# The last stage of a transformer chain merged into the six-layer stage, and cross-attention products on four row groups

## What is computed

```python
# six layers, 16 heads of 8, context of 77 tokens
for i in range(6):
    x = x + attn(rope(adaln(x) @ q), rope(adaln(x) @ k), adaln(x) @ v) @ so      # self
    x = x + attn(rope(adaln(x) @ cq), rope(context @ ck), context @ cv) @ co     # cross
    x = x + gelu(adaln(x) @ f1 + b1) @ f2 + b2
# last block, on h = layernorm(x) of that sum
scores = sigmoid(h @ gate_w)                     # 64 experts in 8 groups
# the best 4 groups, of them the best 8 experts; weights normalised, times 2.5
y = sum_e w_e * ((silu(h @ Wg_e) * (h @ Wu_e)) @ Wd_e)  + shared expert
x = x + y
```

## Time and profile before

| | us |
|---|---|
| median of 3 runs | 2892.53 (2888.77 to 2898.36) |
| the profiled execution's own time | 2894.29 |
| its span | 2892.5 |
| TensorE busy | 2426.3 (84%), mean granted clock 0.856 |
| VectorE, ScalarE busy | 1662.8 (57%), 1171.5 (41%) |
| stage C, about 1100 to 2642 | 1542 |
| stage D with store, 2642 to the end | 251 |

### The profile page before, as it was taken

One profiled execution on the slowest core, in us unless ns is written; L12 is line 12 of the kernel. 1 busy time (PEld: TensorE's weight loads), 2 busy tenths in 40 slices (PEclk: granted clock), 3 DMA queues, 4 the chain that ended last, 5 costly groups with the idle time before them and its releaser, 6 DMA issues. The chain is left out here.

```text
span 2892.5 us, 32350 instructions
## 1 busy us (share of the span) xinstructions
PE 2426.3 (84%) x11288; PEld 956.9 (33%) x11288; DVE 1662.8 (57%) x3709; ACT 1171.5 (40%) x1984; POOL 148.1 (5%) x143
## 2 busy tenths in 40 slices
PE   5999788789996974888888989889798888874799
PEld 2333243433332651233223233222322323222244
DVE  4666758346565576764674574576458347622544
ACT  2333232112222332563655466365456537622121
POOL 0000000011110012000000000000000000001000
PEclk9999988679997896896888699598879859955899
DMA  3000000200000011000100010010001000002000
GB/s 131 1 1 0 1 1 0 103 1 1 1 1 1 1 43 44 23 1 22 39 1 23 1 39 1 22 39 1 23 1 39 1 22 23 1 0 91 0 1 8
DMA packets 38098, 54.35 MB, mean 19 GB/s; under 512 B 5137, under 2 KB 34610, under 8 KB 36402
## 3 DMA queue, kind: packets, MB, share of 16 engines
q1 hardware_dynamic: 37938, 52.28, 5.7%
HBM read 32.34 MB, written 0.52 MB: 11 GB/s over the span
## 5 line engine op out<-in xcount | busy, mean ns | idle before, releaser
L2175 DVE TENSOR_REDUCE C_nm<-ps 128x1 f32<-128x512 f32 x768 | 501.0, 685 | 260.0 <-PE ps L1675 257.6
L2034 ACT ACTIVATE C_prob<-ps 128x512 f32<-128x512 f32 x768 | 430.2, 594 | 198.7 <-PE ps L1695 193.7
L1675 PE MATMUL ps<-C_ks,C_qs 62*128 62x512 bf16 x768 | 275.3, 439 | 52.7 <-DVE C_nm L2175 34.4
L1695 PE MATMUL ps<-C_qs,C_ks 64*128 64x512 bf16 x768 | 256.8, 408 | 43.3 <-ACT C_prob L2034 40.0
L1710 PE MATMUL ps<-C_prob,C_va 128*32 128x512 f32 x1536 | 218.4, 642 | 6.3 <-ACT C_prob L2034 6.3
L2127 ACT ACTIVATE C_u<-ps,C_biasx 77x512 f32<-77x512 f32 x192 | 120.8, 678 | 162.2 <-PE ps L1818 161.8
L1814 PE MATMUL ps<-C_qx,C_kc 32*77 32x512 f32 x384 | 160.6, 922 | 15.2 <-ACT C_u L2127 11.2
L1675 PEld LDWEIGHTS ps<-C_ks,C_qs 62*128 62x128 bf16 x768 | 59.8, 96 | 273.0 <-DVE C_nm L2175 173.0
L714 DVE TENSOR_REDUCE A_nm<-ps 128x2 f32<-128x1024 f32 x64 | 77.6, 1212 | 112.5 <-PE ps L497 112.4
L1695 PEld LDWEIGHTS ps<-C_qs,C_ks 64*128 64x128 bf16 x768 | 56.7, 94 | 255.8 <-ACT C_prob L2034 182.2
L1791 PE MATMUL ps<-C_kc,C_qx 32*128 32x308 f32 x384 | 98.8, 593 | 31.4 <-DVE C_nmx L2266 13.7
(11 more groups left out here) (366 smaller groups left out, 3972.7 us busy)
## 6 DMA issues: line engine op xcount, KB each, us to landing
C_qs<-C_parts SPq DMA_DIRECT2D x72, 128.0 KB, 2.4
C_ks<-C_parts SPq DMA_DIRECT2D x72, 128.0 KB, 2.4
C_w<-in_C_w SPq DMA_DIRECT2D x6, 1090.0 KB, 5.2
D_w<-in_D_ew SPq DMA_DIRECT2D x8, 768.0 KB, 11.4
B_w<-in_B_ew SPq DMA_DIRECT2D x8, 514.0 KB, 10.7
normw_later<-in_norm_w SPq DMA_DIRECT2D x1, 2304.0 KB
A_w<-in_A_w SPq DMA_DIRECT2D x2, 1024.0 KB, 11.9
A_w<-in_A_w SPq DMA_DIRECT2D x2, 768.0 KB, 8.3
```

The costliest lines, as they stand in the source:

```text
L1675: pe.matmul(ps[:, S_BANK + hp, :], lhsT=qs[side(hp, MAX_ROW), b, 2 * q + pq, t * P:(t + 1) * P], rhs=ks[side(hp, MAX_ROW), b, 2 * q + pq, ...
L1695: pe.matmul(ps[:, ST_BANK + hp, :], lhsT=ks[side(1 - hp, HALF), b, 2 * q + pq, kt * P:(kt + 1) * P], rhs=qs[side(1 - hp, HALF), b, 2 * q + ...
L2034: act.activation(prob[:, kt % 2, pq, 1 - hp, :], ps[:, ST_BANK + hp, :], ACT.Exp, scale=SCALE)\
L2175: dve.tensor_reduce(nm[:, q % 2, t, pq, hp:hp + 1], ps[:, S_BANK + hp, :], AX.X, ALU.max, negate=True).then_inc(max_done, 1)
```

## The change

1. Stage D as a stage is gone. `experts_plan` makes a list of extra steps with slots, and `merged` sorts them into the queues of TensorE, ScalarE and VectorE among the units' steps. For batch 0 they start right after unit 10's `FEED_BACK` on VectorE: residual add and norm as one step, then router in 12 parts, gates, and from 300 slots on an expert step every 30 slots; unit 11 ends 913 slots after unit 10. Batch 1's norm and router start after unit 11's `FEED_BACK`, its experts after batch 0's last. Each batch runs its 33 steps by itself; gate, up, spread and down use one bank each: 2, 3, 4 and 1.
2. Memory is shared: `qs`, `ks`, `va` become one buffer `attn`, into which the expert weights are loaded (two DMAs of eight pairs for each batch's half, each after the last weighing of unit 10 or 11). Router tiles lie in `first`, `cos`, `sin`; expert products in `prob`. SP issues these loads after all its other work. GpSimd builds `d.sel` ahead of unit 11's `VX`.
3. `cross_max` and `cross_T` take four row groups at once: 4 steps of four products each in place of 8 of two. r = 0 and 1 go to the banks of `scores` (0, 1) or `scores_T` (2, 3), the others to the ring; in unit 11 only r = 0 does. The heads are laid out anew (`headx`), so that an Exp group of four is one `weigh_x`.
4. `apply` moves from ScalarE to VectorE, as `tensor_scalar` with mean and rstd; the step that made `m.lnu` goes.
5. Banks 0 to 3 are counted by `filled` and `emptied` as the ring is. The slot tables are new throughout, `WINDOW` is 1214.

```diff
-WINDOW = 1155
+WINDOW = 1214
@@ tables, excerpts (b = 0, then b = 1) @@
-     "MAX_X": [1845, 1871, 1895, 1911, 1931, 1949, 1973, 1989],
-     "ST_X": [2048, 2069, 2091, 2124, 2159, 2188, 2222, 2262],
+     "MAX_X": [1935, 1974, 2007, 2047],
+     "ST_X": [2105, 2141, 2200, 2379],
...
-     "ST_X": [1786, 1808, 1829, 1858, 1886, 1923, 1951, 1982],
+     "ST_X": [1898, 1950, 2017, 2080],
@@ VECTOR @@
-     "FEED_BACK": [2572],
+     "FEED_BACK": [2715],
...
-     "FEED_BACK": [2295],
+     "FEED_BACK": [2414],
@@ SCALAR, b = 1 @@
-     "EXP_X": [1800, 1821, 1843, 1872, 1900, 1937, 1964, 1996],
+     "EXP_X": [1923, 1975, 2031, 2094],
...
-     "GELU": [2198, 2219, 2227, 2237],
+     "GELU": [2318, 2340, 2348, 2356],
@@ new @@
+D_STRIDE = 30
+D_EXPERTS = 300
+STEPS_D = PAIR_D + 1
+def experts_plan():
+    last = [(UNITS - B + b) * WINDOW + VECTOR[b]["FEED_BACK"][0] for b in range(B)]
+    plan = {"PE": [], "ACT": [], "DVE": []}
+    begin = 0
+    for b in range(B):
+        at = last[b]
+        plan["DVE"].append((at + 6, "norm", b, 0))
+        plan["PE"].append((at + 66, "turn_norm", b, 0))
+        plan["ACT"].append((at + 76, "copy_norm", b, 0))
+        plan["PE"].append((at + 84, "logits", b, 0))
+        plan["ACT"].append((at + 94, "sigmoid", b, 0))
+        for i in range(ROUTE_PARTS):
+            plan["DVE"].append((at + 104 + 14 * i, "route", b, i))
+        plan["PE"].append((at + 104 + 14 * ROUTE_PARTS, "turn_gates", b, 0))
+        for half in range(2):
+            plan["DVE"].append((at + 114 + 14 * ROUTE_PARTS + 28 * half, "split_gates", b, half))
+        begin = max(begin, at + D_EXPERTS)
+        for e in range(STEPS_D + 1):
+            place = begin + e * D_STRIDE
+            plan["PE"].append((place, "step", b, e))
+            if e < STEPS_D:
+                plan["ACT"].append((place + 10, "silu", b, e))
+                plan["DVE"].append((place + 20, "step", b, e))
+        begin += STEPS_D * D_STRIDE + 4
+        plan["DVE"].append((begin + 16, "take_sum", b, 0))
+        plan["PE"].append((begin + 24, "turn_sum", b, 0))
+        plan["DVE"].append((begin + 32, "add_sum", b, 0))
+    return plan
@@ cross_T (cross_max alike, with S_BANK and 4 * CTX columns) @@
-                    banks = [fill(("stx", c, i, gh)) for gh in range(2)]
+                    banks = [take(("stx", c, q, r), (ST_BANK if c < UNITS - 1 else S_BANK) + r) for r in range(fixed(c))]
+                    banks += [fill(("stx", c, q, r)) for r in range(fixed(c), 4)]
+                    for r in range(4):
+                        rows = slice(32 * r, 32 * r + 32)
+                        pe.matmul(ps[0:CTX, banks[r], :], lhsT=cross.k[rows, c, q, :], rhs=qx[rows, :],
                                   start=True, stop=False)
@@ one expert step on TensorE @@
+                    if k:
+                        pe.wait_ge(silu_done, k)
+                    pe.matmul(ps[0:rows_d(e), GATE_BANK, :], lhsT=gate, rhs=d.hT[:, b, :], start=True, stop=True)\
+                        .then_inc(gate_done, 1)
+                    if k:
+                        pe.wait_ge(mid_done, k)
+                    pe.matmul(ps[0:rows_d(e), UP_BANK, :], lhsT=up, rhs=d.hT[:, b, :], start=True, stop=True)\
+                        .then_inc(up_done, 1)
...
+                        pe.wait_ge(h_ready, k)
+                        half, pair = divmod(e - 1, PAIR_D // 2)
+                        pe.matmul(ps[:, WB_BANK, :], lhsT=d.sel[:, pair, :], rhs=d.gT[:, half, b, :],
+                                  start=True, stop=True).then_inc(wb_done, 1)
@@ weights on SP @@
+                for b in range(B):
+                    sp.wait_ge(pv_done, (UNITS - B + b + 1) * 16)
+                    for i in range(2):
+                        part = slice((2 * b + i) * PAIR_D // 4, (2 * b + i + 1) * PAIR_D // 4)
+                        sp.dma_start(ew[:, part, :, :], a["D_ew"][part].rearrange("e p k d -> p e k d"))\
+                            .then_inc(d_w_loaded[b], 16)
@@ VectorE @@
+                def apply(n, count):
+                    for t in range(TB):
+                        k = n % B * TB + t
+                        ins = dve.tensor_scalar(m.xn[:, k, :], m.y[:, k, :], m.mv[:, t, 0:1], m.rs[:, t:t + 1],
+                                                ALU.subtract, ALU.mult)
```

More of the change, by code:

```diff
@@ new lines, in merged, with router_memory, some @@
+def merged(tables, extra):
+    both = [(at, 0, (n, s)) for at, n, s in timeline(tables)] + [(at, 1, what) for at, *what in extra]
+    return [(kind, what) for at, kind, what in sorted(both, key=lambda x: (x[0], x[1]))]
+def router_memory(flat, first, small, prob):
+    d = Mem()
+    d.hT = flat[:, 0:2 * S].rearrange("p (b s) -> p b s", b=B)
+    d.gT = flat[0:96, 2 * S:4 * S].bitcast(BF16).rearrange("p (h b s) -> p h b s", h=2, b=B)
+    d.sel = flat[0:96, 4 * S:6 * S].bitcast(BF16).rearrange("p (e d) -> p e d", d=P)
+    d.scores, d.sc, d.masked, d.erest, d.wd, d.top = \
+        (flat[:, 6 * S + i * TB * E_D:6 * S + (i + 1) * TB * E_D].rearrange("p (t e) -> p t e", t=TB) for i in range(6))
+    d.rem = prob[0:64, 1, 1, 1, :]
+    d.gw, d.gb = small[:, 0:E_D], small[:, E_D:2 * E_D]
+    at = 2 * E_D
+    def some(n):
+        nonlocal at
+        at += TB * n
+        return small[:, at - TB * n:at].rearrange("p (t n) -> p t n", t=TB)
+    d.gs, d.gtop, d.grest, d.gmask, d.off, d.etop, d.wsum = (some(n) for n in (16, 8, 16, G_D, G_D, 8, 1))
+    d.st, d.mv = some(6), some(2)
+    d.lnv, d.lnt, d.lnu, d.rs = (some(1)[:, :, 0] for _ in range(4))
+    d.ws = first[:, 0:3 * P].rearrange("p (k d) -> p k d", d=P)
+    return d
@@ L1594, in stage_c @@
         prob = sb("prob", [P, 2, 2, 2, S])
+        d = router_memory(first, cos, sin, prob)
+        eg, emid, eh = (prob[:, i // 2, i % 2, :, :] for i in range(3))
+        eacc = prob[:, 1, 1, 0, :]
         shared = sb("u", [P, 8, S])
@@ L1909, in _ @@
+                for late, what in merged(TENSOR, plan["PE"]):
+                    if late:
+                        last_stage(*what)
+                    else:
+                        step(*what)
             @block.sync
@@ L2011, in step @@
                             .then_inc(bias_added, 1)
-                for one in (qs, ks):
-                    pool.memset(one[:].bitcast(F32), 0.0).then_inc(consts_set, 1)
+                for b in range(B):
+                    pool.memset(attn[:, b, 0:8 * S], 0.0).then_inc(consts_set, 1)
                 pool.memset(cross.sel[:], 0.0).then_inc(sel_made, 1)
@@ L2269, in step @@
                     if s in at["SPLIT_MAX_X"]:
-                        for k in range(16):
-                            drained(dve, ("sx", n, k // 2, k % 2))
+                        drained(dve, ("sx", n, TB - 1, 3))
                         if n:
@@ L2562 @@
+                for late, what in merged(VECTOR, plan["DVE"]):
+                    if late:
+                        last_stage(*what)
+                    elif what[0] or what[1] not in early:
+                        step(*what)
+                for b in range(B):
+                    drained(dve, ("da", b))
 def kernel(**inputs):
```

884 lines of the change are left out of this document (447 added, 437 removed), and 58 rows, old and new, of tables (SCALAR, TENSOR, VECTOR).

## The result

| | before | after |
|---|---|---|
| median | 2890.65 us (2874.39 to 2898.36, 4 runs) | 2754.43 us (2752.18 to 2760.86, 4 runs) |
| ratio | | 0.954 (0.950 to 0.958) |
| profiled execution, its span | 2894.29, 2892.5 | 2760.86, 2759.1 |
| mean granted clock | 0.856 | 0.898 |

The forecast was 2743, range 2660 to 2820. The time lies in the range, 11 us above the forecast. What each term of the sum was worth is another question, and for the half of the gain that lies in the six layers the answer is a different one than the prediction gave.

What follows compares the result with a forecast made beforehand. TensorE was taken to bound the slow cross-product stretches at about half clock, sharing the bound with VectorE between them. Span 2892.5 less 85 (tail) less 66 (by T0, unit 10's end) gave 2741.5; forecast 2743, range 2660 to 2820.

Steps and rivals of the forecast that it cites:

- T0 to the first gated expert: From unit 10's end (T0), batch 0's norm and router plus unit 11's VectorE work: first gated expert at T0 + 38.
- Unit 11's end: Unit 11 among 20 of batch 0's expert steps, with 13 us of table-change stalls: ends at T0 + 127.
- Batch 1's router beside 13 steps: Batch 1's norm and router beside batch 0's last 13 expert steps: VectorE's 40 us sets the length, ending T0 + 167.
- Experts of batch 1 and the closing: Batch 1's 33 expert steps alone at 2.79 us, TensorE bound: 92 us, then 6.5 us of closing.
- The tail: From unit 10's end (T0) to the end of the span: 266 us instead of 351.4, 85 us less.
- The cross products: Cross attention on four row groups in the layers: 24.6 us of TensorE a layer saved, 20 of it reaching the end.
- rival A: Full clock returns in the layers' slow cross-product stretches: another 15 us a layer, 83 in all, 2660; chance 0.14.
- Apply: The layers' norm apply moved from ScalarE to VectorE: costs 3 us a layer on the path.
- The coupling: Cross steps in the layers take the other unit's score banks and ring banks: costs 5 us a layer.
- B: The layers' loop gains nothing or loses: 2809, or 2879 if slots were time; chance 0.17.
- C: Emptying the banks after the cross steps becomes the bound, slower: 2924; chance 0.05.
- D: Stalls between experts and unit 11 leave the tail only 30 to 45 us gained: 2785 to 2800; chance 0.06.

Runs made afterwards that it cites:

- e4: The kernel after with Silu replaced by a plain copy in the first 20 expert steps (output not the reference's): 2742.64 us, ratio 0.953.
- v2: The kernel after with Silu of the first 20 expert steps made from Tanh, and the last stage's norm queued in three parts: 2737.81 us, ratio 0.949.
- e1: The kernel after with batch 0's last stage started behind unit 11 in place of unit 10: 2784.85 us, ratio 0.967.
- e6: The kernel after with r = 2 and 3 of each cross step reading the array rows of r = 0 and 1: 3003.85 us, ratio 1.041.
- e3: The kernel after with the norm's apply back on ScalarE, at the same slots: 2815.54 us, ratio 0.977.
- e8: The kernel before with only apply moved from ScalarE to VectorE, at the same slots: 2903.94 us, ratio 1.007.
- a0: The kernel after, unchanged, measured and profiled a second time: 2746.19 us, ratio 0.952 to the kernel before.
- v5: v2 with the rsqrt of the layers' norms refined twice in place of three times: 2747.38 us, ratio 0.952.
- e7: The kernel after with four unused activations (1.65 us together) added on ScalarE at each norm's place, 36 times: 2794.98 us, ratio 0.968.
- e2: The kernel after with the four products of each cross step issued as two and two: 2747.45 us, ratio 0.955.

## Why the prediction held, step by step

**T0 to the first gated expert**: T0 + 38 expected. The shared expert's gate starts at T0 + 31, the first gated pair at T0 + 37 (2514.19): on time. The second starts at T0 + 44.

**Unit 11's end**: T0 + 127 expected, T0 + 130 measured, with the 14 table changes foreseen among the experts. At e4's 0.8 they cost 11 us, not 13.

**Batch 1's router beside 13 steps**: 40 us expected, 50.6 measured. This is the step of the tail that failed. I summed VectorE's work (38.07 us busy in the rows above, so the sum was right) and let nothing stand between. But the norm of batch 1 lies on VectorE in one piece. TensorE's next up product waits until the expert product behind that norm has freed its bank:

```profile
2612.42 1.11 DVE L127 TENSOR_SCALAR xn<-x,C_sin 128x128 f32<-128x128 f32 x4
2613.77 0.69 DVE L2639 TENSOR_TENSOR C_prob<-C_prob,ps 128x512 f32<-128x512 f32 x1 [0.24 <-DVE xn L127]
...
2614.52 1.13 PE L2012 MATMUL ps<-C_first,C_attn 128*128 128x512 f32 x2 [3.70 <-DVE C_prob L2639]
...
2617.30 1.91 PE L2008 MATMUL ps<-C_first,C_attn 128*128 128x512 f32 x2
```

TensorE stands for 3.7 us, and the gate product after it takes 1.91 us for 1.02: the pause was followed by the lower clock level. In all it waits five times for such a product here, 6.9 us together, the others behind parts of the router. The sum of one engine is a lower bound where two engines hand banks to each other. v2 got 4.6 us of this back.

**Experts of batch 1 and the closing**: 92 + 6.5 expected, 101.2 measured, of which the 33 steps are 93. The closing is hardly shorter than with two batches.

**The tail** therefore came to 281.9 us, not 266. My account of it was also incomplete: e1 shows 38 us for the cover, 16 for what became shorter inside unit 11 and 15 for the last stage's new form.

**The cross products**: 24.6 us a layer expected; the four lines now take 63.6 + 49.0 + 23.5 + 18.9 = 155 us in all, 25.8 a layer. Before it was 60.4 in the layer of the earlier trace rows and 58.4 in the mean of all six, so 33 to 35 us of busy time are gone, part of them by the clock. The work saved was sized well (10 us a layer at full speed, about 20 at half). What I gave a chance of 0.14 and left out of the sum, rival A, came for one of the two cross attentions: batch 0's now runs at full clock. That and not the products is most of the 27 us of TensorE time, and e6 shows that it hangs on the four row groups.

**Apply**: the term was 3 us a layer against the change. In the new order it is 12.1 us a layer for it (e3), in the old one 3 to 5 against it (e8). The step that failed is that I priced it by the time it adds to VectorE alone and put at nothing the 9.9 us a layer (6 x 1.65) that leave ScalarE. In the new order these stood before Exps that TensorE needs: e3's idle time grew by 5.4 us, with 4.4 more of waits for Exps, 1.2 more of waits for the transposes' input and the others a little less. The rest of the 12.1 is the clock.

**The coupling**: 5 us a layer taken, 12.1 us more idle time of TensorE measured. By what ended the waits, before and after, a layer has for the self attention's row maxima 4.5 and 8.9 us, for its Exps 7.7 and 11.2, for the transposes' input 1.9 and 5.7 (all of it now at the layer's first norm, 5.7 us each time), for the cross maxima 1.9 and 4.3. So the term failed in size, and a third of it isn't coupling by banks but a norm at which the new order leaves TensorE nothing else to do. That this idle time is what kept rival A from showing in full is argued, not shown.

**The first layers**: not in the sum. Unit 0 ends at 1324.40 after and 1312.44 before, though both start its norm at about 1100: 12 us lost. From 1100 us on TensorE is idle for 46 us in both and busy for 178 after and 167 before, at a clock of 0.82 for 0.87, so the loss is clock and not waiting. With b = 0's ends put back, all of batch 1's self attention, with its context and output, now precedes them, where part of it followed. That this order causes the loss is argued, not shown.

So 66 us by T0 against 63.8 measured was right by cancelling: -12 for the first unit, 75.8 gained in five layers (15.2 each, not 12), where clock gained, idle time lost, and apply had the other sign. Which execution was recorded matters too: in a0 T0 comes 76.9 us earlier than before, so that 63.8 lies so close to 66 is luck. Rivals B, C and D didn't occur: no layer is longer, and cross steps of four are not bound by their evacuation.

What stays open: e6 removes four row groups from an order of work that was made for them, so its 258 us are not what the edit gave in the old order; no kernel with the old tables and four groups was run. Nor was any of TensorE's 41 us of idle time in a layer taken away by an edit, but for the 0.5 us of v5.

## What to carry to other kernels

Where a slow stretch of TensorE is at the lower clock, count what an edit does to busy time times clock and to the clock separately: here work fell by 10 us a layer, and the clock gave more. In a planned in-order kernel the price of work is set by what stands behind it in its queue: 1.65 us put before an Exp that TensorE needs cost its time and more, 0.6 us taken from a chain for which TensorE doesn't wait gave nothing. So look first for what the bounding engine waits for, and don't take a chain that became longer for the cause: the reader may have come late. When long work is put beside short steps that hand banks over, break it into parts, since the sum of one engine's work holds only if the other never has to stand.

## What was unexpected of the hardware

- The same TensorE work, 170 us at full speed a layer, took 186.8 us (a0) or 193.6 (e3) beside 5.4 us more of pauses: each us of pause came with more than one of lower clock. In e7's profiled execution it was 193.4 beside 4.1.
- With batch 0's cross products on two row groups the stretch has a clock of 0.65 though TensorE is busy for 90% of it (61.10 of 68 us, e6); with the same products on four groups it is 1.00, busy 83% (41.29 of 50 us). Batch 1's on two groups are at 0.50, busy 89%. Busy share alone doesn't tell the clock.
- The order in the program doesn't decide whether row groups run side by side: 43.7 and 44.0 us for the same 256 products (e2).
- Tanh needs no load after Exp or after Gelu: from 2516.69 on there is one load for Exp, one for Gelu at 2574.69, and none of their own for the Tanh steps between them and the first Silu (v2). A table change cost 0.8 us of unit 11, less than its load (e4).
